# A selective scan and a quantized MLP on one core: the products by B of every fourth step of two batches move from GpSimd to TensorE

## The chip, the core and the metric

One core of a Trainium2 chip. The time of a run is the device time of the core in microseconds (us); the kernel before took 718.27 us, the median of three runs. Engines are named as in the profile: PE is TensorE (matmuls and transposes), PEld its weight loads, DVE is VectorE, ACT is ScalarE, POOL is GpSimd, SP issues the DMAs.

## What is computed

Four sequences of 512 positions, 512 channels. A block of the Mamba kind reads `ctx_1024` and is gated by the normalized `x`; its result is added to `x`, and then an MLP with quantized activations and ternary weights follows. The part that this change touches is the scan:

```python
x = silu(conv(ctx @ in_proj_w.T) + conv_b)               # u: [4, 512 channels, 512 positions]
dt_low, B, C = split(x_proj_w @ x, [16, 16, 16])         # B, C: [4, 16, 512]
dt = softplus(dt_proj_w @ dt_low + dt_proj_b)
A = -exp(A_log)                                          # [512 channels, 16 n]
state = state * exp(dt * A) + (dt * u) * B               # for each channel and n, along the positions
y = sum over n of state * C
x = x + tanh(g_xattn) * (y + D * u) * silu(layernorm(x))
x = x + tanh(g_ffn) * bitlinear(silu(bitlinear(n, w1)) * bitlinear(n, w2), w3)   # n = layernorm(x)
```

## The kernel before

The scan is cut into 128 steps, 32 to a batch; step k works on one block of 128 x 1024 numbers. In batches 0 and 1 a block is 128 channels, two n and all 512 positions. Batches 2 and 3 are "split" (`SPLIT`): a block is 128 channels, four n and half of the positions (256); the first 16 steps of such a batch do the first half, and `where_split` tells which half h, which group of channels q and which four n, k % 4 being the number of the four. In the second half a scan is issued in four pieces that start from the kept state `hl`.

A step has five stages, each on one engine:

- `times_b` (POOL, L680 in split batches, L686 else): dt*u times B into one of six buffers `hh`. It waits until `sums` of the step six before has read that buffer (`s_sum`).
- `exp` (ACT, L708 in split batches, L713 else): exp(dt*A) into one of two PSUM buffers `dbank` ("da"). It waits until the scan of the step two before has read it (`s_scan`). In the first half of a split batch column 0 of each of the four rows is zero; it is written once per buffer (L705).
- `scan` (DVE, L735 in pieces, L738 whole): reads da and hh, writes hh in place.
- `times_c` (POOL, L752 in split batches, L757 else): hh times C, in place.
- `sums` (PE, L787): eight transposes of hh by the identity, added up in `bank_y`; at the first step of a group the product D * u is added (L778). `gate` (DVE, L561, L570) then takes `bank_y`.

No scheduler orders the work. Each engine runs a loop over 125 slots that is written out by hand; the number of the slot says what each engine issues: in slot k POOL does `times_c(k)` and `times_b(k + 4)`, ACT `exp(k + 4)`, DVE `scan(k + 3)`, PE `sums(k - 1)`, each in its place among the other work. An engine goes through its instructions in order, so a wait holds back all that is behind it.

The other work is the front of the next batch (projection, convolution: L227, L302, L389 to L406), `dt_scalar` (ACT, softplus, with an ACT table load before it and another before the next exp), `du_vector` (DVE, L327) for a pair of groups in the slots of `PAIR`, the gates z, and above all the MLP of 128 rows each, the tiles. A tile starts in slot u (`tile_slot`), every six slots from slot 70 on. Its path over the engines is: rows centred (ACT, L845) and scaled (DVE, L856 and what follows; ACT, L887), transposed (PE, L904; ACT, L911), then in slots u to u + 3 for each of four chunks c `ab_tensor` (PE, L936, L942), tanh (ACT, L956), two products (DVE, L963, L971) and a square (ACT, L977). From slot u + 4 on: maximum (DVE, L1002), a power on POOL (L1033), scaling (ACT, L1029); in slots u + 8 and u + 9 `ht_tensor` turns a piece (PE, L1080), `hqt_scalar` copies it out of the one bank `bank_t` (ACT, L1091), four times in turn; in slot u + 10 `out_tensor` (PE, L1111) and `out_vector` (DVE, L1118). `ab_tensor(c + 1)` waits for the first DVE product of chunk c.

Of the places of slots one matters below: slot u + 3 of a tile holds, on PE, `sums`, then `ht_tensor` 2 and 3 of the tile before, then `ab_tensor` of chunk 3 (slots 79, 91, 103 and 115 are such slots).

## Time and profile before

| what | value |
|---|---|
| median of three runs | 718.27 us (718.25 to 718.8) |
| the profiled execution: its own time | 717.76 us |
| its span, first to last instruction | 716.0 us |
| mean granted clock of TensorE | 0.889 of full speed |
| POOL busy | 625.4 us (87%), 300 instructions |
| DVE busy | 605.9 us (85%), 839 instructions |
| ACT busy | 515.4 us (72%), 971 instructions |
| PE busy | 512.1 us (72%), 2562 matmuls |

The span is 1.76 us shorter than the time of the same execution, and that execution is 0.51 us under the median. Times in the rows below count from the first instruction of the span. A PE row's "x4" counts records: a matmul on float32 leaves two, a transpose or an fp8 matmul one.

The two split batches are steps 64 to 127; in this execution they run from about 356 us (the first `times_c` of step 64 starts at 354.8) to 669 us. What follows until 716 us is the end of the last three tiles, with no scan in it.

### The profile page before, as it was taken

The page shows a single profiled execution, that of the slowest core. Times are in us where ns is not written, and L with a number is a line of the kernel's source. Part 1 is how long each engine was busy: PE and PEld are TensorE (multiplying, and loading weights), DVE is VectorE, ACT ScalarE, POOL GpSimd, SP SyncE. Part 2 cuts the span into 40 slices and gives each one's busy share as a digit, 9 for nine tenths or more (in the row PEclk, how much of TensorE's full clock was granted, in tenths as well). Part 3 has the DMA queues.
Part 4 walks back from the last instruction along what each step waited for, and adds up shares of the span by engine and source line. Part 5 has one row for each costly group of instructions (what it writes and reads, how often), then busy time and mean ns, then how long its engine had stood idle before and what let it go on. Part 6 is the DMA issues. An engine that isn't in the chain of part 4 may idle for free.

```text
span 716.0 us, 8124 instructions
## 1 busy us (share of the span) xinstructions
PE 512.1 (72%) x2562; PEld 314.2 (44%) x2562; DVE 605.9 (85%) x839; ACT 515.4 (72%) x971; POOL 625.4 (87%) x300
## 2 busy tenths in 40 slices
PE   9787889556451758787575668578686876758897
PEld 3243434223441435555353435345453544445554
DVE  7679778977999898988868888999889889888865
ACT  5844866159867868868677777898788797677653
POOL 1499999979999999999999999988998899988431
PEclk9999999969556998999785979899999998989999
DMA  4695875258950000037310000027510000000001
GB/s 169 217 402 209 305 293 211 89 181 333 413 238 15 6 29 2 29 125 266 125 61 19 31 0 16 1 82 250 197 70 6 15 2 16 0 16 16 1 16 44
DMA packets 23930, 80.78 MB, mean 113 GB/s; under 512 B 2432, under 2 KB 4608, under 8 KB 20816
## 3 DMA queue, kind: packets, MB, share of 16 engines
q1 hardware_dynamic: 23888, 80.27, 30.7%
q8 instruction: 20, 0.33, 0.2%
q14 instruction: 22, 0.18, 0.1%
HBM read 72.53 MB, written 7.73 MB: 112 GB/s over the span
## 4 chain that ended last, share of the span: by engine, by line
DVE 29%; ACT 21%; PE 21%; POOL 13%; issue 11%; DMA 3%; SPq 1%; DVEq 0%; ACTq 0%; POOLq 0%
DVE hh L738 7%; ACT da L708 5%; DVE hh L735 4%; POOL hh L686 4%; POOL hh L757 4%; PE bank_y L787 3%; PE bank_a L936 3%; PE bank_t L1080 3%; DMA wq<-x 2%; PE bank_b L942 2%; POOL hh L680 2%; POOL hh L752 2%; ACT room L1091 2%; DVE sm L640 2%; ACT room L977 2%
## 5 line engine op out<-in xcount | busy, mean ns | idle before, releaser
L738 DVE TENSOR_TENSOR_SCAN hh<-da,hh 128x1024 f32<-128x1024 f32 x96 | 217.5, 2277 | 6.7 <-POOL hh L686 3.5
L787 PE MATMUL bank_y<-ident,hh 128*128 128x128 f32 x1024 | 146.4, 293 | 25.0 <-POOL hh L757 19.3
L757 POOL TENSOR_TENSOR hh<-hh,cc 128x1024 f32<-128x1024 f32 x64 | 160.3, 2505 | 2.4 <-DVE hh L738 2.4
L787 PEld LDWEIGHTS bank_y<-ident,hh 128*128 128x128 f32 x1024 | 130.0, 152 | 54.9 <-POOL hh L757 27.9
L752 POOL TENSOR_TENSOR hh<-hh,cc 128x1024 f32<-128x1024 f32 x64 | 151.3, 2364 | 3.1 <-ACT hl L721 2.0
L686 POOL TENSOR_TENSOR hh<-pair,bb 128x1024 f32<-128x1024 f32 x30 | 71.6, 2388 | 26.0 <-DMA bb<-xd_scratch 25.8
L735 DVE TENSOR_TENSOR_SCAN hh<-da,hl,hh 128x256 f32<-128x256 f32 x128 | 85.0, 728 | 0.0
L680 POOL TENSOR_TENSOR hh<-wq,bb 128x1024 f32<-128x1024 f32 x32 | 75.6, 2361 | 10.7 <-PE bank_y L787 10.7
L686 POOL TENSOR_TENSOR hh<-wq,bb 128x1024 f32<-128x1024 f32 x32 | 76.6, 2395 | 3.4 <-PE bank_y L787 3.4
L680 POOL TENSOR_TENSOR hh<-pair,bb 128x1024 f32<-128x1024 f32 x32 | 75.6, 2363 | 3.4 <-PE bank_y L787 3.4
L302 PE MATMUL bank_b<-room 128*128 128x512 f32 x96 | 47.4, 640 | 24.8 <-DVE wq L406 23.2
L713 ACT ACTIVATE da<-wq,cst 128x511 f32<-128x511 f32 x64 | 41.5, 684 | 28.4 <-DVE hh L738 28.3
L708 ACT ACTIVATE da<-wq,cst 128x256 f32<-128x256 f32 x128 | 53.3, 466 | 11.7 <-DVE hh L735 9.4
L708 ACT ACTIVATE da<-pair,cst 128x255 f32<-128x255 f32 x128 | 53.1, 463 | 10.9 <-DVE hh L738 10.9
L713 ACT ACTIVATE da<-pair,cst 128x511 f32<-128x511 f32 x64 | 41.3, 680 | 22.8 <-DVE hh L738 22.8
L1091 ACT ACTIVATE room<-bank_t,sm 128x512 bf16<-128x512 f32 x53 | 36.2, 683 | 28.5 <-PE bank_t L1080 28.4
L963 DVE SCALAR_TENSOR_TENSOR room<-room,bank_a 128x512 f32<-128x512 f32 x52 | 35.4, 681 | 24.5 <-ACT room L956 23.9
L936 PE MATMUL bank_a<-wq,room 128*128 128x512 fp8e4 x120 | 36.6, 434 | 16.6 <-DVE room L963 16.4
L956 ACT ACTIVATE room<-bank_a,sm 128x512 f32<-128x512 f32 x58 | 39.3, 677 | 11.3 <-PE bank_a L936 11.3
L1111 PE MATMUL bank_t<-wq,room 128*128 128x512 fp8e4 x192 | 43.4, 379 | 0.0
L936 PE MATMUL bank_a<-wq,xqT 128*128 128x512 fp8e4 x112 | 33.8, 431 | 11.7 <-DVE room L963 10.9
L302 PEld LDWEIGHTS bank_b<-room 128*128 128x128 f32 x96 | 18.6, 204 | 46.6 <-issue 37.1
(250 smaller groups left out, 1046.5 us busy)
## 6 DMA issues: line engine op xcount, KB each, us to landing
bb<-xd_scratch SPq DMA_DIRECT2D x32, 512.0 KB, 5.2
cc<-xd_scratch SPq DMA_DIRECT2D x32, 512.0 KB, 7.7
wq<-weights SPq DMA_DIRECT2D x12, 1024.0 KB, 6.5
stage<-weights SPq DMA_DIRECT2D x8, 1024.0 KB, 6.7
xin<-x SPq DMA_DIRECT2D x4, 1024.0 KB, 5.5
room<-weights SPq DMA_DIRECT2D x4, 1024.0 KB, 9.8
u_scratch<-wq SPq DMA_DIRECT2D x6, 512.0 KB, 3.4
wq<-x SPq DMA_DIRECT2D x2, 1024.0 KB, 18.5
```

The source lines that it names most:

```text
L302: mm = pe.matmul(bank_b[:, :], diag_w[:, e, k, :], xpad[e % 2][:, k:k + L], start=(k == 0), stop=(k == TAPS - 1))
L680: ins = g_.tensor_tensor(quarters(flat(hh[k % NH])), du2[g % 4][:, HALF * (q % 2):HALF * (q % 2 + 1)].unsqueeze(1).to_broadcast([P, 4, HAL ...
L686: ins = g_.tensor_tensor(hh[k % NH][:, :, :], du2[g % 4].unsqueeze(1).to_broadcast([P, GN, L]), bb[:, s * GN:(s + 1) * GN, :], ALU.mult)
L708: ins = act.activation(da[:, j, first:HALF], dt2[g % 4][:, HALF * (q % 2) + first:HALF * (q % 2 + 1)], ACT.Exp, scale=a_neg[:, q, n + j:n ...
L713: ins = act.activation(dbank[k % 2][:, j, 1:L], dt2[g % 4][:, 1:L], ACT.Exp, scale=a_neg[:, q, s * GN + j:s * GN + j + 1])
L735: ins = v.tensor_tensor_scan(h[:, t], flat(dbank[k % 2])[:, t], h[:, t], hl[:, q, n + j:n + j + 1], ALU.mult, ALU.add)
L738: ins = v.tensor_tensor_scan(h, flat(dbank[k % 2]), h, 0.0, ALU.mult, ALU.add)
L752: ins = g_.tensor_tensor(quarters(flat(hh[k % NH])), quarters(flat(hh[k % NH])), cc[:, n:n + 4, t], ALU.mult)
L757: ins = g_.tensor_tensor(hh[k % NH][:, :, :], hh[k % NH][:, :, :], cc[:, s * GN:(s + 1) * GN, :], ALU.mult)
L787: mm = pe.matmul(bank_y[:, (first + c) * P:(first + c + 1) * P], flat(hh[k % NH])[:, at:at + P], ident[:, :], start=False, stop=(s == STEP ...
L936: mm = pe.matmul(a[:, :], xqT[i % 2][:, k, :], w1q[:, k, c * 512:(c + 1) * 512], start=(k == 0), stop=(k == NE - 1))
L1091: MA.did(act.activation(hqT[:, 4 * g:4 * g + 4, :].rearrange("p a b -> p (a b)"), bank_h(i, g)[:, :], ACT.Identity, bias=nmagic), ("hqT", ...
```

## The change

In both split batches the steps with k % 4 = 3 (the n from 12 to 15, 16 steps in all) get their product dt*u*B from PE:

- `times_b` is not issued for these steps; PE does `times_b_tensor` at the start of the slot k - 4, ahead of `sums`. It is four float32 matmuls into `dbank`, 256 columns each: the stationary operand is dt*u turned (positions by channels), the moving one two diagonal matrices of B.
- `exp` of these steps goes into the buffer `hh`, and the scan reads the exponentials from `hh` and the product from `dbank`. `exp` therefore waits for `sums` of six steps before, not for the scan of two steps before. The matmuls wait for that scan (`s_scan, k - 1`).
- Each group g from 8 on is turned once (`TURN`): four PE transposes into `bank_b` or `bank_a`, one ACT copy to SBUF. The buffer of one turned group is one of the four of u; u is then loaded one group at a time into three.
- The diagonals (`DIAG`): 32 ACT copies of the identity, 128 x 128, each scaled by a column of B, into the place in `bb` that held rows 12 to 15 of the broadcast B; these rows are loaded no more (four DMAs of 512 KB less). The columns of B come from four transposes and a small ACT copy per batch (`cols`).
- Column 0 is zeroed again in every odd step of a first half.
- The softplus of groups 10 and 11 moves from slot 66 to slot 69.

The core of the diff:

```diff
-PAIR = {2: 25, 3: 37, 4: 49, 5: 66, 6: 87, 7: 99}
+PAIR = {2: 25, 3: 37, 4: 49, 5: 69, 6: 87, 7: 99}
+LAST_N = NS - 4
+TURN = {8: 62, 9: 64, 10: 75, 11: 81, 12: 93, 13: 93, 14: 105, 15: 111}
+DIAG = {(2, 0): (60, 60, 60, 61, 61, 61, 62, 62), (2, 1): (64, 65, 66, 67, 68, 69, 70, 71),
+        (3, 0): (80, 81, 82, 83, 84, 85, 86, 87), (3, 1): (96, 97, 98, 99, 100, 101, 102, 103)}
+def by_tensor(k):
+    return split(k) and k % 4 == 3
...
+        def diagonal_scalar(act, b, h, i):
+            n, c = LAST_N + i % 4, 2 * h + i // 4
...
+            CA.did(act.activation(bb[:, n, c * P:(c + 1) * P], ident[:, :], ACT.Copy,
+                                  scale=b_cols[b][:, c, i % 4:i % 4 + 1]), ("diag", b, h, i))
...
+        def turn_tensor(pe, g):
+            pe.wait_ge(*GV.of(("du", g)))
...
+            for c in range(NE):
+                mm = pe.transpose(turn_bank(g)[:, c * P:(c + 1) * P], du2[g % 4][:, c * P:(c + 1) * P], ident[:, :])
+            CP.did(mm, ("duT", g))
+        def turn_scalar(act, g):
+            act.wait_ge(*CP.of(("duT", g)))
...
+            CA.did(act.activation(duT[g % 2], turn_bank(g)[:, :], ACT.Copy), ("duT", g))
+        def times_b_tensor(pe, k):
+            b, h, q, n = where_split(k)
+            g = k // STEPS
+            pe.wait_ge(s_scan, k - 1)
+            pe.wait_ge(*CA.of(("duT", g)))
+            pe.wait_ge(*CA.of(("diag", b, h, 7)))
+            for c in range(2):
+                at = 2 * (q % 2) + c
+                for j in range(2):
+                    mm = pe.matmul(dbank[k % 2][:, j, :].rearrange("p (n t) -> p n t", n=2)[:, :, c * P:(c + 1) * P],
+                                   duT[g % 2][:, at * P:(at + 1) * P],
+                                   bb[:, n + 2 * j:n + 2 * j + 2, HALF * h + c * P:HALF * h + (c + 1) * P],
+                                   start=True, stop=True)
+            CP.did(mm, ("m1", k))
...
         def exp(act, k):
-            if k >= 2:
+            if by_tensor(k):
+                act.wait_ge(s_sum, k - NH + 1)
+            elif k >= 2:
                 act.wait_ge(s_scan, k - 1)
...
-                da = quarters(flat(dbank[k % 2]))
-                if k % PER < 2:
+                da = quarters(flat(hh[k % NH] if by_tensor(k) else dbank[k % 2]))
+                if h == 0 and (k % PER < 2 or k % 2):
                     act.activation(da[:, :, 0], zero4[:, :], ACT.Copy)
...
         def scan(v, k):
+            elif by_tensor(k):
+                v.wait_ge(*CP.of(("m1", k)))
...
+            da, m1_ = (h, flat(dbank[k % 2])) if by_tensor(k) else (flat(dbank[k % 2]), h)
...
-                    if k + LEAD < ALL:
+                    if k + LEAD < ALL and not by_tensor(k + LEAD):
                         times_b(g_, k + LEAD)
...
                 for k in range(SLOTS):
+                    if by_tensor(k + LEAD):
+                        times_b_tensor(pe, k + LEAD)
                     if 0 <= k - 1 < ALL:
                         sums(pe, k - 1)
```

How it moves instructions, in three places. First PE in slots 90 and 91, which are slots u + 2 and u + 3 of the tile that starts in slot 88 (`xqT1` is its turned input, `room` and `wq` are the tile before and the weights; `hh5` and `hh0` are `sums` of steps 89 and 90). Before:

```order
L787 MATMUL bank_y<-ident,hh5 128x128 x8
L1080 MATMUL bank_t<-ident,room 128x128 x8
L936 MATMUL bank_a<-wq,xqT1 128x512 x4
L942 MATMUL bank_b<-wq,xqT1 128x512 x4
L787 MATMUL bank_y<-ident,hh0 128x128 x8
L1080 MATMUL bank_t<-ident,room 128x128 x8
L936 MATMUL bank_a<-wq,xqT1 128x512 x4
```

Now:

```order
L876 MATMUL bank_y<-ident,hh5 128x128 x8
L1172 MATMUL bank_t<-ident,room 128x128 x8
L1028 MATMUL bank_a<-wq,xqT1 128x512 x4
L1034 MATMUL bank_b<-wq,xqT1 128x512 x4
L390 MATMUL da1<-bb,wq 128x2x128 x4
L876 MATMUL bank_y<-ident,hh0 128x128 x8
L1172 MATMUL bank_t<-ident,room 128x128 x8
L1028 MATMUL bank_a<-wq,xqT1 128x512 x4
```

The four matmuls of L390 (step 95) stand between chunk 2 of the tile and all that PE does in slot 91; the row with x8 after `sums` is `ht_tensor` 2 and 3.

Second, POOL around the same slots. Before, `times_c` of steps 90 to 92 (L752) and `times_b` of steps 94 to 96 (L680; step 95 goes into hh5):

```order
L752 TENSOR_TENSOR hh0<-hh0,cc 128x1024
L680 TENSOR_TENSOR hh4<-wq,bb 128x1024
L752 TENSOR_TENSOR hh1<-hh1,cc 128x1024
L680 TENSOR_TENSOR hh5<-wq,bb 128x1024
L752 TENSOR_TENSOR hh2<-hh2,cc 128x1024
L680 TENSOR_TENSOR hh0<-pair,bb 128x1024
```

Now:

```order
L841 TENSOR_TENSOR hh0<-hh0,cc 128x1024
L764 TENSOR_TENSOR hh4<-wq,bb 128x1024
L841 TENSOR_TENSOR hh1<-hh1,cc 128x1024
L841 TENSOR_TENSOR hh2<-hh2,cc 128x1024
L764 TENSOR_TENSOR hh0<-pair,bb 128x1024
```

`times_b(95)` is gone; `times_c` of steps 91 and 92 stand next to each other.

Third, ACT in slots 82 to 84: the scaled columns and rows of the next tile (L845; L934 now), the copy L532 (L616 now), then a tanh and an exp for each slot. Before:

```order
L845 ACTIVATE gbuf<-room,sm 128x512 x2
L532 ACTIVATE gbuf<-bank_t,sm 128x512
L956 ACTIVATE room<-bank_a,sm 128x512
L708 ACTIVATE da1<-wq,cst 128x256 x4
L1029 ACTIVATE wq<-wq,sm 128x1024 x2
L977 ACTIVATE room,sm<-room 128x512
L956 ACTIVATE room<-bank_a,sm 128x512
```

Now:

```order
L934 ACTIVATE gbuf<-room,sm 128x512 x2
L616 ACTIVATE gbuf<-bank_t,sm 128x512
L354 ACTIVATE bb<-ident,sm 128x128
L1048 ACTIVATE room<-bank_a,sm 128x512
L794 ACTIVATE hh3<-wq,cst 128x256 x4
L1121 ACTIVATE wq<-wq,sm 128x1024 x2
L1069 ACTIVATE room,sm<-room 128x512
L354 ACTIVATE bb<-ident,sm 128x128
L1048 ACTIVATE room<-bank_a,sm 128x512
```

A diagonal (L354) stands at the end of each of these slots, ahead of the next tanh; the exponentials of step 87 go to hh3.


## Rows read from the trace of the kernel before

**Rows 1.** The page's busy time of each engine over the whole span: us (share), instructions.

```profile
PE 512.1 (72%) x2562; PEld 314.2 (44%) x2562; DVE 605.9 (85%) x839; ACT 515.4 (72%) x971; POOL 625.4 (87%) x300
```

**Rows 2.** Stretches: length, then PE, PEld, DVE, ACT, POOL busy (count), clock, DMA share, GB/s.

```profile
330.00:477.00 147.00, 100.64 (x559) 67.71 (x557) 124.52 (x188) 112.77 (x252) 144.09 (x67) 0.84 0.15 50
356.00:667.00 311.00, 222.14 (x1248) 146.12 (x1248) 271.60 (x433) 246.54 (x544) 291.80 (x137) 0.89 0.13 46
574.10:577.50 3.40, 3.03 (x8) 1.11 (x9) 3.20 (x3) 3.40 (x7) 3.40 (x3) 0.50 0.02 5
```

**Rows 3.** Waits from 356 to 667 us: who waited for whom, us, times, longest.

```profile
DVE room L963 <- ACT room L956: 15.1, 17, 1.5
POOL hh L680 <- PE bank_y L787: 14.1, 9, 3.4
ACT da L708 <- DVE hh L735: 9.4, 6, 2.7
...
DVE wq L327 <- ACT bank_a L319: 5.9, 1, 5.9
PE bank_y L787 <- POOL hh L752: 4.1, 1, 4.1
DVE sm L1016 <- POOL sm L1033: 1.3, 1, 1.3
```

**Rows 4.** The chain that ended last, 356 to 667 us, its largest shares by engine and line.

```profile
by line: issue 13.0%; ACT da L708 11.1%; DVE hh L735 10.2%; POOL hh L680 5.1%; POOL hh L752 4.9%; PE bank_t L1080 4.0%; PE bank_a L936 3.6%; PE bank_y L787 3.5%; ACT room L1091 3.3%; ACT room L977 3.2%; ACT room L956 3.0%; DVE hh L738 2.9%;
```

**Rows 5.** The chain in order of time, in slots 78, 79 and 82: start, us, what.

```profile
428.88 1.71 PE bank_b L942 x4
430.58 1.01 PE bank_y L787 x8
...
450.26 0.58 ACT room L956
```

**Rows 6.** Groups, 356 to 667 us: count, busy us, mean ns of one, idle before.

```profile
L680 POOL TENSOR_TENSOR hh<-wq,bb 128x1024 f32<-128x1024 f32 x32 | 75.6, 2361 | 10.7 <-PE bank_y L787 10.7
L708 ACT ACTIVATE da<-pair,cst 128x255 f32<-128x255 f32 x112 | 46.5, 463 | 7.2 <-DVE hh L738 7.2
L505 ACT ACTIVATE gbuf<-xin,sm 128x256 f32<-128x256 f32 x16 | 9.5, 592 | 0.2
L506 ACT ACTIVATE bank_a<-xin,sm 128x256 f32<-128x256 f32 x16 | 8.9, 553 | 0.0
L532 ACT ACTIVATE gbuf<-bank_t,sm 128x512 f32<-128x512 f32 x8 | 5.3, 668 | 0.0
L705 ACT ACTIVATE da<-zero 128x4 f32<-128x4 f32 x2 | 0.4, 176 | 1.1 <-DVE hh L735 1.1
```

**Rows 7.** The same view of the whole span: exponentials of 511 columns.

```profile
L713 ACT ACTIVATE da<-pair,cst 128x511 f32<-128x511 f32 x64 | 41.3, 680 | 22.8 <-DVE hh L738 22.8
```

**Rows 8.** PE in order of time: four float32 matmuls of 256 columns, then the next.

```profile
365.51 1.03 PE L276 MATMUL bank_a<-wq,dtw 128*128 128x256 f32 x4
366.38 1.03 PE L276 MATMUL bank_b<-wq,dtw 128*128 128x256 f32 x4
367.24 0.38 PE L1111 MATMUL bank_t<-wq,room 128*128 128x512 fp8e4 x1
```

**Rows 9.** DVE, PE and ACT in order of time, in slots 90, 91 and 107.

```profile
490.34 2.67 DVE L735 TENSOR_TENSOR_SCAN hh<-da,hl,hh 128x256 f32<-128x256 f32 x4
...
492.93 1.03 PE L942 MATMUL bank_b<-wq,xqT 128*128 128x512 fp8e4 x4
...
494.67 0.60 PE L1080 MATMUL bank_t<-ident,room 128*128 128x128 f32 x4
...
494.04 1.67 ACT L708 ACTIVATE da<-wq,cst 128x256 f32<-128x256 f32 x4
495.64 0.68 ACT L1091 ACTIVATE room<-bank_t,sm 128x512 bf16<-128x512 f32 x1
...
574.47 1.89 PE L936 MATMUL bank_a<-wq,room 128*128 128x512 fp8e4 x4 [2.42 <-DVE room L963]
```

More of the change, by code:

```diff
@@ L156, in build @@
         gates = cst[:, 92:94]
-        col = iter(range(280))
+        col = iter(range(312))
         def small(n=1):
@@ L175, in build @@
         amh, amh_end = small(2), small(3)
+        b_cols = {b: small(16).rearrange("p (a b) -> p a b", a=NE) for b in SPLIT}
         am1, ss1, v2, rh, rk, amhx, ri2, csh = [small() for _ in range(8)]
@@ L193, in build @@
         HA = line("state_scalar")
+        CP, CA = line("turned_tensor"), line("turned_scalar")
         BV, BP = line("first_products"), line("first_rows_of_b")
@@ L312, in x_dbl_scalar, with cols_tensor, cols_scalar @@
             FA.did(act.activation(xd[0:ROWS, :], bank_t[0:ROWS, :], ACT.Copy), ("xd", b))
+        def cols_tensor(pe, b):
+            pe.wait_ge(*FA.of(("xd", b)))
+            for c in range(NE):
+                mm = pe.transpose(bank_t[:, c * P:(c + 1) * P], xd[:, c * P:(c + 1) * P], ident[:, :])
+            FP.did(mm, ("cols", b))
+        def cols_scalar(act, b):
+            act.wait_ge(*FP.of(("cols", b)))
+            FA.did(act.activation(b_cols[b], bank_t[:, :].rearrange("p (a b) -> p a b", a=NE)[
+                :, :, RANK + LAST_N:RANK + NS], ACT.Copy), ("cols", b))
@@ new lines, in turn_bank @@
+        def turn_bank(g):
+            return bank_a if g == 13 else bank_b
+        def turn_tensor(pe, g):
+            pe.wait_ge(*GV.of(("du", g)))
+            if g == 9:
+                pe.wait_ge(*CA.of(("duT", g - 1)))
+            else:
+                tile = max(i for i in range(END) if tile_slot(i) < TURN[g])
+                pe.wait_ge(*MV.of(("g" if g == 13 else "h", tile, NCH - 1)))
+            for c in range(NE):
+                mm = pe.transpose(turn_bank(g)[:, c * P:(c + 1) * P], du2[g % 4][:, c * P:(c + 1) * P], ident[:, :])
+            CP.did(mm, ("duT", g))
@@ new lines, in turn_scalar @@
+        def turn_scalar(act, g):
+            act.wait_ge(*CP.of(("duT", g)))
+            if g == 2 * NE:
+                act.wait_ge(*d_bw.of(("bw", NB - 1)))
+            elif g == 2 * NE + 1:
+                act.wait_ge(s_seed, 2 * NE)
+            else:
+                act.wait_ge(*CP.of(("m1", STEPS * (g - 2) + 7)))
+            CA.did(act.activation(duT[g % 2], turn_bank(g)[:, :], ACT.Copy), ("duT", g))
[13 more added lines that the diff above has]
+            CP.did(mm, ("m1", k))
@@ L663, in m1_done @@
         def m1_done(k):
-            return k - 1
+            return k - 1 - sum(by_tensor(i) for i in range(k + 1))
         def times_b(g_, k):
@@ L923, in ab_tensor @@
                     pe.wait_ge(*GV.of(("du", 2 * pair_before(i) + 1)))
+                for g in TURN:
+                    if 0 < i <= END and tile_slot(i - 1) < TURN[g] < tile_slot(i):
+                        pe.wait_ge(*CA.of(("duT", g)))
             if i == END and c == 1:
@@ L1139, in weight_part, with u_before, load_u @@
                     return weights[i // 4][:, (i % 4) * WC:(i % 4 + 1) * WC]
[L1141 to L1145 removed]
+                def u_before(g):
+                    return g - 3 if g > 2 * NE + 2 else g - NE
+                def load_u(g):
+                    b, n = g // NE, g // 2
+                    sp.wait_ge(s_seed, u_before(g) + 1)
+                    sp.wait_ge(*GV.of(("du", u_before(g))))
                     for half in d_uw:
                         sp.wait_ge(*half.of(b))
[L1148 to L1154 removed]
+                    if b in SPLIT:
+                        h, p = n % 2, g % 2
+                        d_u[n % 2].did(sp.dma_start(u_of(g).rearrange("p (a b) -> p a b", a=2),
+                                                    u_dram[b, :, 2 * p:2 * p + 2, HALF * h:HALF * (h + 1)]), n)
+                    else:
+                        d_u[n % 2].did(sp.dma_start(u_of(g), u_dram[b, :, g % NE, :]), n)
                 def load_dt_rows(b):
@@ L1225, in _ @@
                             load_dt_rows(b)
-                    for n in PAIR:
-                        if k == 16 * n - 20:
-                            load_u(n)
+                    for g in range(NE, NB * NE):
+                        if k == (8 * g - 20 if g % 2 == 0 else 8 * g - 28 if g < 10 else 8 * g - 22):
+                            load_u(g)
                     for i in range(NW):
@@ L1255, in _ @@
                         for s in range(STEPS):
-                            if k == last_use(b - 1, s) - LEAD + 1:
+                            if k == last_use(b - 1, s) - LEAD + 1 and not (b in SPLIT and s >= LAST_N // GN):
                                 load_bb(b, s)
@@ L1350, in _ @@
                             x_dbl_scalar(act, b)
+                        if k == FRONT[b] + 10 and b in SPLIT:
+                            cols_scalar(act, b)
                     for i in range(NW):
@@ L1385, in _ @@
                             z_turn_scalar(act, i)
+                    for g in TURN:
+                        if k == TURN[g]:
+                            turn_scalar(act, g)
+                    for b, h in DIAG:
+                        for i in range(8):
+                            if k == DIAG[b, h][i]:
+                                diagonal_scalar(act, b, h, i)
                     if k == 9:
@@ L1471, in _ @@
                             out_tensor(pe, i)
+                    for b in SPLIT:
+                        if k == FRONT[b] + 10:
+                            cols_tensor(pe, b)
                     for i in TILES:
@@ L1474, in _ @@
                             z_turn_tensor(pe, i)
+                    for g in TURN:
+                        if k == TURN[g]:
+                            turn_tensor(pe, g)
                     for i in range(END + 1):
```

42 lines of the change are left out of this document (22 added, 20 removed).

## The prediction

> **What bounds the kernel now.** The busy shares come first [rows 1]: POOL leads with 87%, DVE follows with 85%, so on that view the change takes work from the right engine. The two split batches are the stretch from 356 to 667 us [rows 2]: POOL is busy 291.8 of 311 us (94%), DVE 271.6 (87%), ACT 246.5 (79%), PE 222.1 (71%). The reader is to see two things there: POOL has hardly any idle time, and no engine below it has much either.
>
> A busy engine need not be a waited-for engine, so the waits come next [rows 3]. In these 311 us DVE waits for POOL once, 1.3 us, in the power of a tile, not in a scan. PE waits for POOL once, 4.1 us. POOL in turn waits 14.1 us in nine places for `sums` on PE, before just the instruction that the change removes. DVE's long waits are on ACT (15.1 us in 17 places before the first product of a chunk), and ACT's on DVE. POOL runs without gaps because its buffers let it follow, not because others stand in line for it.
>
> The chain that ended last says the same by another road [rows 4]: of the named shares POOL has 5.1 + 4.9 = 10.0% of 311 us, 31 us; ACT, DVE and PE share nearly all the rest in turn. My reading: **the tile path over PE, ACT and DVE, tied to the scans by program order, sets the end of the split batches, and POOL keeps up with it.** So what is taken from POOL is worth little, and what is put on PE or ACT counts where the chain passes.
>
> **The change part by part.** The sum is made against the profiled execution, 717.76 us; the median of the runs shown lies 0.51 us above it.
>
> *Products off POOL.* 16 instructions of 2.36 us [rows 6] are 37.8 us less on POOL. What others wait for POOL is 1.3 and 4.1 us [rows 3], so the gain is between 0 and 5.4 by that view; the far end is rival A. I take 1.3: PE, after its wait of 4.1, has no tile work ready. **-1.3.**
>
> The Trainium skill has a rule that would give another sum: its page Perfetto Trace Analysis, section Identifying the Most-Contended Engine, takes the engine of highest occupancy as the bottleneck, to be relieved first. By that rule this step alone would give the gain of rival A, and the trace, in which the others hardly wait for this engine, speaks against it.
>
> *Products on PE.* Four float32 matmuls of 256 columns. L276 does the same four in 367.24 - 365.51 = 1.73 us, at full clock [rows 8]. 16 times this is 27.7 us more on PE; at the lower clock, twice that. The bounds on the path are 0 and 27.7 (55 with every one at half clock). Where they stand on the path: in slot 79 the chain goes on PE from `ab_tensor` straight to `sums` [rows 5], and the products go between: +1.73. In slot 91 `ht_tensor` 2 ends at 494.67 + 0.60 = 495.27 and ACT takes it at 495.64, after its exponentials [rows 9]; with 1.73 ahead it ends at 497.00, and the copy, `ht_tensor` 3, chunk 3 and its tanh come 1.36 later. Slots 103 and 115 have the same pattern. 1.73 + 3 x 1.36 = **+5.8**. In the other slots PE's next tile work waits for something that ends later, so I take nothing. The wait for the scan does not bind in slot 91: that scan ends at 490.34 + 2.67 = 493.01, PE is free at 492.93 + 1.03 = 493.96 [rows 9]. Behind the products on PE stand `sums`, the transposes and chunk 3; for `sums` POOL waits, which now has 2.36 us to spare.
>
> *Clock.* From 574.1 to 577.5 the granted clock is 0.50, that is 1.2 GHz [rows 2]; before it PE waits 2.42 us for DVE, and the four matmuls then take 1.89 us, against 1.03 for four of the kind in slot 90 [rows 9]. In slot 107 the products fill this gap: chunk 1 starts about 0.8 later and, if the clock stays up, ends about 1.6 sooner over its two banks. **-0.8**; the bounds are +0.8 and, should several such stretches go, some -4.
>
> *Diagonals.* 511 columns take 680 ns [rows 7], 255 take 463 [rows 6]: 0.85 ns a column, so 128 columns are about 355 ns. Four exponentials follow each other in 1.67 us [rows 9], some 0.06 us each less than their records; a diagonal holds ACT for about 0.30. Eight stand in slots 60 to 62, before the stretch; 24 stand in it, 0 to 8.5 us. On the path: where the chain stays on ACT past the end of a slot, as from slot 82 to 83 [rows 5]; I count six such ends. 6 x 0.30 = **+1.8**.
>
> *Small additions on ACT.* 14 more zeroings of 176 ns [rows 6], of which three on the path: +0.5. Exponentials into SBUF: a 256-column activation takes 592 ns there and 553 into PSUM [rows 6], so 64 x 0.04 = 2.5 us at most; I take 0.5. Eight copies of a turned group at 668 ns [rows 6], and as many times four transposes at 0.60 [rows 9]: 0 to 10; most fall where ACT waits for a scan, I take one copy, 0.7. Together **+1.7**.
>
> *At nothing.* The wait of 16 `exp` on a scan goes; a quarter of 9.4 us [rows 3] would be 2.4, but in slot 91, the pattern slot, `exp` starts as soon as tanh is done, so the scan is not what ends its wait. The next thing that could be late is the scan itself, which now waits for PE: products done at about 495.7 in slot 91, a slot ahead of their scan. The softplus of groups 10 and 11 moves three slots: DVE's wait of 5.9 us for it [rows 3] goes from its place and comes back three slots on, with the same table loads; 0, bounds -5 and +3. The columns of B are small, and four DMAs fewer relieve queues that nothing here waits for.
>
> Sum: -1.3 + 5.8 - 0.8 + 1.8 + 1.7 = +7.2, so 725.0 for the profiled execution and **725.5** for the median.
>
> **The rivals.**
>
> *A, faster: POOL is the bound after all.* Place: 330 to 477 us, where POOL is busy 144.1 of 147 us and DVE has 22 us to spare [rows 2]. Mechanism: the chain shows only the wait that ends last; DVE and ACT may run at just POOL's pace because everything is tied through `sums` and the buffers. Six of the sixteen products were issued there, in slots 63 to 83: 6 x 2.36 = 14.2 us, hence 703.6, a median near 704. It decides if additions to PE and ACT stay below about 7 us on the path and DVE can use the time. For it: the near-absence of gaps on POOL. Against it: one wait on POOL of 1.3 us on DVE's side, none in a scan worth the name.
>
> *B, much slower: PE becomes the bound.* Each group of products stands at the head of a slot and waits for a scan, so the transposes and chunks behind it slip each time; 12 more of them at 1.73 on the path are +20.8, about 746. It decides if the slip of one slot is still there when the next product comes, four slots on. Against it: PE is at 71% and has its own gaps.
>
> *C, no change.* The relief in the stretch of A and the additions after it cancel: 718 within 1.4 us. For it: both sums are of like size.
>
> **How the numbers follow.** About 0.2% (1.4 us) is what a measurement of this kernel can tell from no change. Forecast 0.46, A 0.33, B 0.08, C 0.13. Faster 0.33; same 0.13; slower 0.46 + 0.08 = 0.54. The range: upward the forecast's own, where products, diagonals and turned groups take about half of their upper bounds, to 737; it leaves out B. Downward A, with some room below its 704, to 702; it leaves out the tenth in which more than six products pay. The likeliest case's own range is 719 to 737.
>
> **What would show it.** Right: POOL's busy time falls by about 38 us and its idle time in the split batches grows by as much or more; that stretch gets no shorter; on the chain POOL's share falls, and L390 (products) and L354 (diagonals) appear between PE and ACT pieces; in slots u + 3 the copy after `ht_tensor` 2 comes over a microsecond later than tanh and exponentials would allow. Products take about 1.73 us a group at full clock. Wrong: steps between 330 and 477 us at well under the 4.7 us of two POOL operations [rows 6], which would be A; or scans that wait for L390, which I have put at nothing; or stretches at half clock that vanish in numbers.

## The result and the profile after

The changed kernel takes 729.87 us, median of four executions (726.21 to 730.86), beside 718.26 us for the kernel before on the same chip: a ratio of 1.0153 [1.0135, 1.0171]. It is slower, by 11.6 us; the prediction was 725.5 us in a range of 702 to 737, with slower the likeliest outcome. A second set of six executions (run 10) has a median of 726.25 us, 7.9 us over the kernel before; all ten together have 727.9. The profiled execution is one of 730.16 us, its span 728.4 us, the mean granted clock 0.892.

The page's busy times, which answer to [rows 1]:

```profile
PE 545.4 (75%) x2730; PEld 345.4 (47%) x2730; DVE 607.1 (83%) x839; ACT 530.6 (73%) x1027; POOL 589.1 (81%) x284
```

POOL is busy 36.3 us less, PE 33.3 us and ACT 15.2 us more, DVE as before. The stretches follow, with the columns of [rows 2]: first the split batches, then three stretches at half clock.

```profile
356.00:679.00 323.00, 248.99 (x1394) 173.19 (x1393) 270.38 (x430) 258.38 (x587) 255.29 (x120) 0.91 0.12 42
453.30:460.10 6.80, 6.08 (x18) 4.70 (x19) 5.44 (x13) 6.33 (x13) 2.21 (x2) 0.50 0.00 0
525.00:531.80 6.80, 5.93 (x20) 3.88 (x21) 6.44 (x7) 4.78 (x14) 4.21 (x2) 0.50 0.26 92
555.70:562.50 6.80, 5.58 (x19) 3.46 (x20) 6.26 (x10) 6.15 (x14) 5.12 (x3) 0.50 0.00 0
```

The split batches took 311 us and take 323. In them POOL is busy 255.3 us instead of 291.8, so its idle time grew from 19 to 68 us, and nothing came of it. The waits of that stretch (who for whom: us, times, longest) show where it sits, beside [rows 3]:

```profile
POOL hh L764 <- PE bank_y L876: 51.8, 21, 4.9
DVE room L1055 <- ACT room L1048: 28.8, 19, 3.4
ACT room L1183 <- PE bank_t L1172: 28.3, 27, 2.7
...
ACT da L794 <- DVE hh L824: 6.6, 5, 2.3
PE da L390 <- DVE hh L827: 6.3, 3, 3.5
...
DVE hh L827 <- PE da L390: 0.5, 1, 0.5
```

POOL's wait for `sums` on PE went from 14.1 to 51.8 us: all that was taken from POOL became waiting for PE. DVE's wait for tanh on ACT in front of a chunk went from 15.1 to 28.8, and ACT's wait for transposes on PE (`ht`, L1172; L1080 before) went from 20.1 to 28.3. A scan waits for the products (L390) once, 0.5 us. The chain that ended last, by line, against [rows 4]:

```profile
by line: DVE hh L824 10.0%; issue 9.6%; PE bank_y L876 6.2%; ACT da L794 5.9%; PE bank_a L1028 5.3%; PE da L390 4.7%; PE bank_t L1172 4.6%; DVE hh L827 4.2%; POOL hh L841 3.8%; PE bank_b L1034 3.8%; ACT room L1183 3.3%; DVE sm L1094 2.8%; P
```

Products on TensorE have 4.7% of 323 us there, 15 us; they are busy for 36.1 us in all (L390 below), so some two fifths of their time is on the path. The groups of the whole span that are new, with POOL's remaining products (columns as in [rows 6]):

```profile
L764 POOL TENSOR_TENSOR hh<-wq,bb 128x1024 f32<-128x1024 f32 x24 | 56.5, 2353 | 32.6 <-PE bank_y L876 32.6
...
L390 PE MATMUL da<-bb,wq 128*128 128x256 f32 x128 | 36.1, 431 | 15.3 <-DVE hh L827 6.3 <-ACT bb L354 5.5 <-DVE hh L824 3.5
...
L794 ACT ACTIVATE hh<-wq,cst 128x256 f32<-128x256 f32 x32 | 13.6, 497 | 0.0
L354 ACT ACTIVATE bb<-ident,sm 128x128 f32<-128x128 f32 x32 | 12.0, 391 | 0.0
```

A product on POOL kept its length, 2353 ns. A diagonal takes 391 ns, an exponential of 256 columns into SBUF 497 ns, where one of 255 into PSUM takes 463 [rows 6].

**Where the time arises.** The same scan can be found in both traces. The start of scan k, us from the start of the span, at the places where the lag jumps:

```
scan      before  after    lag
 69       364.4   365.2    0.82
 74       394.2   396.1    1.87
 82       431.3   433.2    1.88
 83       436.8   440.5    3.74   products of slot 79
 86       452.4   456.2    3.84
 87       457.2   462.8    5.61   products of slot 83
 94       495.5   501.1    5.57
 95       500.4   507.3    6.98   products of slot 91
100       524.0   531.1    7.07
101       528.9   538.4    9.46   525.0 to 531.8 at half clock
105       551.8   561.5    9.75
106       556.8   567.9   11.16   555.7 to 562.5 at half clock
107       561.7   574.2   12.48   products of slot 103
111       580.0   592.6   12.57
112       585.0   598.5   13.54   593.3 to 596.7 at half clock
118       617.0   629.8   12.74
119       621.9   636.0   14.15   products of slot 115
127       664.1   677.6   13.54
```

The four slots of the prediction give 1.9 + 1.4 + 1.3 + 1.4 = 6.0 us, where it had 1.73 + 3 x 1.36 = 5.8. The chain in order of time in slot 91 (start, us, what) shows the mechanism as it was put:

```profile
498.67 0.86 PE bank_b L1034 x4
499.53 1.73 PE da L390 x8
501.26 0.87 PE bank_y L876 x8
502.13 0.45 PE bank_t L1172 x4
...
502.61 0.70 ACT room L1183
```

The products stand between chunk 2's second bank and `sums`, and the copy of the tile's turned piece on ACT (L1183) comes behind all of it. Three other jumps, 1.8 + 2.4 + 1.4 = 5.6 us, were not in the prediction, and half clock is in each. Of the rest, 0.8 us stand before scan 69, and 1.1 us up to scan 74 have no cause shown (run 5); the 1.0 us at scan 112 is for the greater part gone by scan 118. In slot 83:

```profile
451.29 2.69 DVE hh L824 x4
...
454.02 3.78 PE da L390 x8
457.80 1.71 PE bank_y L876 x8
459.51 1.26 PE bank_a L1028 x4
...
460.80 0.70 ACT room L1048
```

The products wait for the scan, then take 3.78 us, where those of slot 91 take 1.73; `sums` takes 1.71 instead of 0.87, and chunk 1 behind it is late too. In slots 96 and 97 no product stands on the chain at all:

```profile
525.87 1.09 PE bank_t L1172 x4
526.96 1.71 PE bank_a L1028 x4
528.66 1.71 PE bank_b L1034 x4
530.37 1.65 PE bank_y L867 x8
```

Transposes, both banks of a chunk and the product D * u (L867) run at half clock, 1.71 us for a bank that takes 0.86 in slot 91. The kernel before has full clock in the same place, which is some 7 us earlier there:

```profile
517.60:524.40 6.80, 4.82 (x32) 3.40 (x32) 6.73 (x8) 5.11 (x14) 6.80 (x4) 1.00 0.19 65
```

### The profile page after: what moved, and what is told of

It is laid out like the page before. It is cut to its first block, busy times and chain, and to the rows that moved or that the text cites. A ratio compares the mean times of both kernels' runs of the same rounds, so it can differ in the third digit from the quotient of the medians.

```text
span 728.4 us, 8552 instructions
## 1 busy us (share of the span) xinstructions
PE 545.4 (75%) x2730; PEld 345.4 (47%) x2730; DVE 607.1 (83%) x839; ACT 530.6 (73%) x1027; POOL 589.1 (81%) x284
## 4 chain that ended last, share of the span: by engine, by line
DVE 29%; PE 27%; ACT 17%; POOL 13%; issue 9%; DMA 3%; SPq 1%; DVEq 0%; ACTq 0%; POOLq 0%
DVE hh L827 7%; POOL hh L846 5%; POOL hh L770 5%; PE bank_y L876 5%; DVE hh L824 4%; PE bank_a L1028 4%; PE bank_t L1172 3%; PE bank_b L1034 3%; ACT da L794 3%; PE da L390 3%; DMA wq<-x 2%; ACT room L1183 2%; DVE sm L724 2%; POOL hh L841 2%; DVE sm L1094 2%
## 5 line engine op out<-in xcount | busy, mean ns | idle before, releaser
L827 DVE TENSOR_TENSOR_SCAN hh<-da,hh 128x1024 f32<-128x1024 f32 x88 | 199.6, 2277 | 6.4 <-POOL hh L770 3.6
L876 PE MATMUL bank_y<-ident,hh 128*128 128x128 f32 x1024 | 145.7, 292 | 15.2 <-POOL hh L846 13.6
L770 POOL TENSOR_TENSOR hh<-pair,bb 128x1024 f32<-128x1024 f32 x30 | 71.6, 2389 | 26.5 <-DMA bb<-xd_scratch 24.9
L764 POOL TENSOR_TENSOR hh<-wq,bb 128x1024 f32<-128x1024 f32 x24 | 56.5, 2353 | 32.6 <-PE bank_y L876 32.6
L770 POOL TENSOR_TENSOR hh<-wq,bb 128x1024 f32<-128x1024 f32 x32 | 76.8, 2400 | 2.6 <-PE bank_y L876 2.6
L764 POOL TENSOR_TENSOR hh<-pair,bb 128x1024 f32<-128x1024 f32 x24 | 56.5, 2354 | 19.3 <-PE bank_y L876 19.3
L824 DVE TENSOR_TENSOR_SCAN hh<-da,hl,hh 128x256 f32<-128x256 f32 x96 | 63.9, 729 | 0.0
L1183 ACT ACTIVATE room<-bank_t,sm 128x512 bf16<-128x512 f32 x53 | 36.3, 685 | 35.4 <-PE bank_t L1172 35.3
L1048 ACT ACTIVATE room<-bank_a,sm 128x512 f32<-128x512 f32 x58 | 39.3, 677 | 11.9 <-PE bank_a L1028 11.7
L390 PE MATMUL da<-bb,wq 128*128 128x256 f32 x128 | 36.1, 431 | 15.3 <-DVE hh L827 6.3
L794 ACT ACTIVATE da<-wq,cst 128x256 f32<-128x256 f32 x96 | 39.9, 466 | 6.7 <-DVE hh L824 6.6
L794 ACT ACTIVATE da<-pair,cst 128x255 f32<-128x255 f32 x96 | 39.8, 462 | 6.6 <-DVE hh L827 6.5
L1028 PE MATMUL bank_a<-wq,xqT 128*128 128x512 fp8e4 x112 | 33.3, 426 | 11.9 <-DVE room L1055 11.6
```

Of the source, the lines that this page charges most:

```text
L390: mm = pe.matmul(dbank[k % 2][:, j, :].rearrange("p (n t) -> p n t", n=2)[:, :, c * P:(c + 1) * P], duT[g % 2][:, at * P:(at + 1) * P], bb ...
L764: ins = g_.tensor_tensor(quarters(flat(hh[k % NH])), du2[g % 4][:, HALF * (q % 2):HALF * (q % 2 + 1)].unsqueeze(1).to_broadcast([P, 4, HAL ...
L770: ins = g_.tensor_tensor(hh[k % NH][:, :, :], du2[g % 4].unsqueeze(1).to_broadcast([P, GN, L]), bb[:, s * GN:(s + 1) * GN, :], ALU.mult)
L794: ins = act.activation(da[:, j, first:HALF], dt2[g % 4][:, HALF * (q % 2) + first:HALF * (q % 2 + 1)], ACT.Exp, scale=a_neg[:, q, n + j:n ...
L824: ins = v.tensor_tensor_scan(h[:, t], da[:, t], m1_[:, t], hl[:, q, n + j:n + j + 1], ALU.mult, ALU.add)
L827: ins = v.tensor_tensor_scan(h, da, m1_, 0.0, ALU.mult, ALU.add)
```

## The experiments

Each ran beside the kernel before, whose median was 718.4 to 718.5 us in every set; ratios are to it.

**1. POOL's relief alone.** From the kernel before:

```diff
+def left_out(k):
+    return split(k) and k % 4 == 3
...
-            return k - 1
+            return k - 1 - sum(left_out(i) for i in range(k + 1))
...
+            elif left_out(k):
+                v.wait_ge(s_sum, k - NH + 1)
...
-                    if k + LEAD < ALL:
+                    if k + LEAD < ALL and not left_out(k + LEAD):
```

> The kernel before with the 16 products simply left out on POOL and nothing put in their place (these steps scan what their buffer still holds; the scan waits for sums in their stead). This prices the relief by itself. If POOL only follows the tile path: 1.3 us faster, at most 5.4, so 713 to 718, near 717. If POOL is the bound (rival A): about 14 us faster, near 704.

Measured: 719.28 us, ratio 1.0013 [1.0, 1.0026]: no gain. The split batches and three of their waits:

```profile
356.00:667.00 311.00, 221.94 (x1238) 148.27 (x1239) 269.79 (x430) 245.46 (x542) 254.29 (x120) 0.89 0.13 46
```

```profile
POOL hh L684 <- PE bank_y L793: 34.8, 20, 4.1
...
DVE room L969 <- ACT room L962: 18.0, 18, 2.0
...
DVE hh L744 <- ACT da L712: 0.6, 1, 0.6
```

POOL is busy 37.5 us less, as in the change, and waits for `sums` 34.8 us where it waited 14.1. Rival A (704 us) falls: POOL, at 94% in this stretch, is not what the kernel waits for. The time lies just over the range of the first expectation (713 to 718) and far from the second. It also shows the term of -1.3 us to be nothing. The wait that these scans were given instead hides no gain in this profile: the only wait of a scan in the stretch is one of 0.6 us, for an exponential (L744).

**2. A quarter of each product.** From the changed kernel:

```diff
-            for c in range(2):
+            for c in range(1):
...
-                for j in range(2):
+                for j in range(1):
```

> The changed kernel with one of the four matmuls of each group of products; the other three quarters of the product are left out, all waits stay. 1.30 us less of PE per group. If the time of the matmuls lies on the path at the steps where the scans fell back (in slots 79, 83, 91, 103 and 115 by 1.3 to 1.9 us each, 7.8 together): three quarters of that come back, about 6 us, near 724. If it is the wait of PE for the scan, and not its work, that costs: no change, 729 to 731.

Measured: 720.99 us, ratio 1.0036 [1.0023, 1.0049]: 9 us come back, more than the 6 of the theory (5 us against the second set of the change, run 10). So the time on PE is the greater part of the cost, not the waits, copies or diagonals that stay. Its mean granted clock was 0.888 to 0.898, as low as the change's. That does not clear the clock, for its half-clock stretches are placed otherwise: in its profile they last 3.4 us and not 6.8 in slot 83 and in slots 96 and 97, and the jumps there are 0.5 and 1.4 us instead of 1.8 and 2.4. The run takes away work on PE and half clock in these places together.

**3. The products later in their slots.** From the changed kernel, nothing left out:

```diff
-                    if by_tensor(k + LEAD):
-                        times_b_tensor(pe, k + LEAD)
+                    later = by_tensor(k + LEAD)
...
+                            if later:
+                                times_b_tensor(pe, k + LEAD)
+                                later = False
...
+                    if later:
+                        times_b_tensor(pe, k + LEAD)
```

> The changed kernel, the products moved back within their slot on PE: behind transposes 2 in slots 79, 91, 103 and 115, at the end of the slot in the twelve others. Nothing left out. If their place at the head of the slot is what costs: in slots 83 and 119 chunk 1 no longer stands behind them (1.8 and 1.3 back), in the four others the gap of 1.2 us between transposes 2 and 3 takes most of it (0.8 each back): about 5 us, near 725. If PE's amount of work costs, wherever it stands: no change. If the scans then wait for products: slower than 730.

Measured: 720.88 us, ratio 1.0031 [1.0019, 1.0043]: again 9 us back, with all of the products kept (5 us against the second set of the change). What is left over the kernel before is 2.4 us. Place decides: the same work costs 5 to 9 us more at the head of a slot.

**4. Small diagonals.** From the changed kernel:

```diff
-            CA.did(act.activation(bb[:, n, c * P:(c + 1) * P], ident[:, :], ACT.Copy,
+            CA.did(act.activation(bb[:, n, c * P:c * P + 4], ident[:, 0:4], ACT.Copy,
```

> The changed kernel with diagonals of 4 columns and not 128 (the rest of each diagonal matrix is left out). ACT is held about 0.1 us and not 0.3 by each of the 24 in the split batches. With six of them on the path, as counted before: 1.2 us faster, near 728.5. With all on the path: 4.8 us, near 725.

Measured: 728.68 us, ratio 1.014 [1.0122, 1.0158], 1.2 us under the change's median. The group shows what was saved:

```profile
L354 ACT ACTIVATE bb<-ident,sm 128x4 f32<-128x4 f32 x32 | 8.7, 286 | 0.0
```

286 ns in place of 391, 3.4 us over 32, so most of a diagonal's length is fixed. The gain has the expected size, but the intervals overlap, and run 10 shows the changed kernel itself at 725.4 to 731.6: on the diagonals this one is inconclusive.

Its trace is of use for something else, for all sixteen products stand in it at full length at the head of their slots. Its lag is 2.9 us at scan 64 already, ahead of the split batches, against 0.9 in the change's profile; from scan 74 to scan 127 it grows by 8.8 us, and in the change by 11.7. The stretches at half clock in the places of the three extra jumps:

```profile
455.40:458.80 3.40, 2.98 (x7) 2.45 (x8) 3.26 (x10) 3.40 (x8) 1.39 (x1) 0.50 0.00 0
527.10:530.40 3.30, 3.30 (x13) 2.34 (x12) 3.23 (x5) 3.18 (x11) 2.02 (x1) 0.50 0.13 33
554.40:561.20 6.80, 5.71 (x19) 3.57 (x20) 6.40 (x9) 5.70 (x13) 5.00 (x3) 0.50 0.00 0
```

In the first two places half clock lasts 3.4 us and not 6.8, and the jumps (scans 87 and 101) are 0.4 and 1.3 us instead of 1.8 and 2.4. In the third it lasts as long as in the change, and the jump (scan 106) is 1.4 us in both. So the extra jumps go with the length of the half clock there, with the same products ahead; that the shorter diagonals have a part in it is not ruled out.

**5. The softplus moved alone.** From the kernel before:

```diff
-PAIR = {2: 25, 3: 37, 4: 49, 5: 66, 6: 87, 7: 99}
+PAIR = {2: 25, 3: 37, 4: 49, 5: 69, 6: 87, 7: 99}
...
-                    pe.wait_ge(*ZV.of(("zz", {3: 4, 4: 6, 5: 7, 6: 11, 7: 12}[n])))
+                    pe.wait_ge(*ZV.of(("zz", {3: 4, 4: 6, 5: 8, 6: 11, 7: 12}[n])))
```

> The kernel before, with the softplus pair that the change moves from slot 66 to slot 69 moved alone (and its wait for the z of the next tile); nothing left out. The prediction put this move at 0, with bounds of -5 and +3. The changed kernel's scans gain 4 us at scans 70 to 72 and lose 5 until scan 74, a net of about +1. Theory (a small loss, which belongs to the change): 718.5 to 720, nearest 719.5. Rival (the loss at scan 74 is due to what PE and ACT do there in the changed kernel, and the move by itself is worth nothing or saves some of the 4 us): 714 to 718.

Measured: 718.19 us, ratio 0.9996 [0.9985, 1.0008]. My theory of a small loss falls; the 0 of the prediction stands. The lag of +1.1 us between scans 69 and 74 is not a price of this move: in this run's trace the lag is 1.7 us at scan 69 and 1.6 at scan 74. Where it comes from stays open.

**6. Only four groups later.**

```diff
-                    if by_tensor(k + LEAD):
+                    later = by_tensor(k + LEAD) and k in (79, 91, 103, 115)
+                    if by_tensor(k + LEAD) and not later:
                         times_b_tensor(pe, k + LEAD)
```

(with the lines of run 3 behind the third turn)

> The changed kernel with the products of four slots only (79, 91, 103 and 115, in which PE also turns the third and fourth part of a tile) put behind the third turn; the other twelve groups stay at the head of their slots. Nothing left out. Theory by the prediction's own terms (these four are the 5.8 us): 729.9 - 5.8 = about 724, and what is left to the 720.9 of the kernel with all sixteen put later is the twelve that were taken at nothing (3 us). Rival (the four cost what the scans' steps show, but what they give back is lost in the next tile work, and the twelve matter most): 727 or more.

Measured: 720.42 us, ratio 1.0049 [1.0024, 1.0074]. The interval is wide because the twelve executions lie in two groups: seven of 718.4 to 720.5 us at a mean granted clock of 0.907 to 0.910, five of 724.1 to 726.5 at 0.896 to 0.899. The quicker group is no slower than run 3: there the other twelve products cost nothing at the head of their slots, as the prediction took it. The other five executions are 3 to 6 us over run 3's median, so this does not hold in all of them. The profile is of the quicker group:

```profile
356.00:669.00 313.00, 240.30 (x1397) 167.61 (x1396) 270.64 (x431) 257.68 (x587) 256.03 (x120) 0.93 0.13 43
451.60:455.00 3.40, 3.26 (x8) 2.63 (x9) 3.25 (x10) 3.40 (x8) 1.12 (x1) 0.50 0.00 0
455.00:458.40 3.40, 3.40 (x24) 2.41 (x23) 2.06 (x4) 3.40 (x8) 2.13 (x1) 1.00 0.01 2
519.80:526.60 6.80, 4.82 (x32) 3.40 (x32) 6.73 (x8) 5.50 (x15) 5.43 (x3) 1.00 0.28 75
```

Slot 83's products stand at its head here too (451.7 us) and take 3.57 us at half clock, but full clock is back at 455.0, 3.4 us after it fell and not 6.8; the lag grows by 0.5 us instead of 1.8. The place of slots 96 and 97 (519.8) has full clock, and the jump of 2.4 us is not there.

**7 and 8. Using POOL's freed time.** The rounding of eight tiles (`hq`) from ACT to POOL, on run 3's kernel and on the kernel before:

```diff
+ROUND_POOL = range(4, 12)
...
-                pe.wait_ge(*(MG if at_end(i) or i == END - 1 and g >= 2 else MA).of(("hq", i, g // 2)))
+                pe.wait_ge(*(MG if at_end(i) or i == END - 1 and g >= 2 or i in ROUND_POOL else MA).of(("hq", i, g // 2)))
...
+                    for i in ROUND_POOL:
+                        if k == tile_slot(i) + 7:
+                            hq_pool(g_, i, 0)
+                            hq_pool(g_, i, 1)
...
-                        if k == u + 7:
+                        if k == u + 7 and i not in ROUND_POOL:
```

> The changed kernel with the products put later (720.9), and besides, the rounding of eight tiles (16 ScalarE instructions of 128x1024, 1.23 us each) done by POOL (1.12 us each by the five at the end), at the end of the same slot. Nothing left out. It uses the time that the change freed on POOL (about 37 us) to free 19.7 us on ScalarE. Theory (ScalarE and the chain through it carry a good part of the rest, and POOL has room): 20 to 40 per cent of 19.7 us come back, so 713 to 717, nearest 715, which is under the kernel before. Rival (ScalarE waits for PE in these slots anyway, 21 us before its copies of turned tiles, and the round comes later from POOL because POOL is in the middle of a product): 720 to 724.

> The kernel before with the same rounding of eight tiles done by POOL in place of ScalarE; nothing left out. Here POOL is busy 94 per cent of this stretch and idle for only 19 us, so 18 us more on it leave no slack. Theory (POOL has no room without the change, so the freed time of POOL is what the move needs): POOL becomes the bound and it takes 3 to 10 us more, 721 to 728. Rival (the load on POOL does not decide, as leaving out 38 us of it did not, and the relief of ScalarE is worth the same with and without the change): 712 to 716.

Measured: 717.77 us, ratio 0.9989 [0.9976, 1.0002], with the change; 721.3 us, ratio 1.0039 [1.0024, 1.0054], without it. The same move saves 3 us on the one and costs 2.9 on the other. The chain of the second, 356 to 668 us, and two POOL groups of it:

```profile
by line: POOL hh L753 21.4%; POOL hh L681 19.2%; issue 13.5%; DVE hh L736 9.4%; ACT da L709 4.3%; PE bank_a L937 2.3%; PE bank_t L1081 2.2%; ACT room L1092 1.7%; DVE room L964 1.7%; PE bank_b L943 1.5%; DVE sm L1003 1.5%; POOL wq L1040 1.4%
```

```profile
L681 POOL TENSOR_TENSOR hh<-wq,bb 128x1024 f32<-128x1024 f32 x32 | 75.5, 2358 | 0.0
L1040 POOL TENSOR_SCALAR room<-room,sm 128x1024 f32<-128x1024 f32 x8 | 8.9, 1122 | 3.2 <-DVE sm L1024 3.2
```

Now POOL's two products have 40.6% of the chain, against 10.0% in the kernel before [rows 4], and their idle time for `sums` (10.7 us, [rows 6]) is 0. So 18 us more on POOL make it the bound, though 37.5 us less gave nothing: it was close to being one, and was none. With the change the same groups have room:

```profile
L765 POOL TENSOR_TENSOR hh<-wq,bb 128x1024 f32<-128x1024 f32 x24 | 56.6, 2357 | 4.1 <-PE bank_y L877 4.1
L1132 POOL TENSOR_SCALAR room<-room,sm 128x1024 f32<-128x1024 f32 x8 | 8.9, 1119 | 9.9 <-DVE sm L1116 9.9
```

With the change the time lies between the theory's range (713 to 717) and the rival's, so the theory's size was too good; POOL waits 9.9 us for the scales in front of these eight roundings, and 11.0 in front of the other eight.

**9. Less of it, and more.** Rounding on POOL for tiles 5, 7, 9 and 11 alone (`ROUND_POOL = (5, 7, 9, 11)`), and then the diagonals on POOL too:

```diff
-            CA.did(act.activation(bb[:, n, c * P:(c + 1) * P], ident[:, :], ACT.Copy,
-                                  scale=b_cols[b][:, c, i % 4:i % 4 + 1]), ("diag", b, h, i))
+            DG.did(g_.tensor_scalar(bb[:, n, c * P:(c + 1) * P], ident[:, :], b_cols[b][:, c, i % 4:i % 4 + 1],
+                                    None, ALU.mult), ("diag", b, h, i))
```

> The kernel with the products put later, and the rounding of four tiles (numbers 5, 7, 9 and 11) on POOL in place of all eight. These are the tiles whose rounding falls into a slot from which the change took the POOL product (83, 95, 107, 119), so there the two roundings of 1.12 us each take the place of a product of 2.36 us; the other four go back to ScalarE, for POOL waited 21 us in front of the roundings for their scales with all eight. Nothing left out. Theory (only the freed slots have room on POOL): at least as good as with all eight, 715.5 to 717.5, nearest 716.5. Rival (each of the eight pays in the same way by what it takes off ScalarE): half of the 3 us, 719 to 719.5.

> The same kernel with the 32 diagonals of B made by POOL in place of ScalarE (391 ns each there, 12.5 us; with four columns in place of 128 they cost the changed kernel 1.2 us less). Nothing left out. Theory (POOL still has room, so what the diagonals cost on ScalarE comes back): 1 to 2 us under the kernel without this, so 714.5 to 716. Rival (POOL has no more room in the slots where they fall, two or three at a time in slots 60 to 62, with its products at their full number until 66): 0 to 2 us more, 716.5 to 719.

Measured: 719.2 us, ratio 0.9998 [0.9983, 1.0013], and 720.43 us, ratio 1.0014 [0.9991, 1.0036]. By the ratios four tiles save 2.4 us against run 3 and eight 3.0, with intervals that reach 1 us to either side, so whether the freed slots are what counts stays open. The median, 719.2, lies in the rival's range (719 to 719.5) and not in the theory's. With the diagonals on POOL the median is over both ranges, and its executions lie in two groups, four of 714.6 to 716.8 us at 0.911 to 0.912 and eight of 720.0 to 722.8 at 0.903 to 0.910. No gain of the diagonals is measured there, at 609 ns each:

```profile
L355 POOL TENSOR_SCALAR bb<-ident,sm 128x128 f32<-128x128 f32 x32 | 19.4, 609 | 0.0
```

No version of these is measurably quicker than the kernel before.

**10. Only four groups first, and the change again.** The counterpart of run 6 (`k not in (79, 91, 103, 115)` for the ones put later), and more executions of the changed kernel:

> The counterpart of the last but one pair: the four groups of slots 79, 91, 103 and 115 stay at the head of their slots, as in the change, and the other twelve go to the end of theirs. Nothing left out. Theory (the four cost the 5.9 us that the scans show, and the rest of the 9 us is time at half clock, which comes and goes with where the twelve stand): 725.5 to 727.5, nearest 726.7 = 720.9 + 5.8. Rival (the four carry all of it, by whatever way): 729 to 730.5, as the changed kernel.

> The changed kernel itself, with more executions (there are four so far: 726.2 at a mean granted clock of 0.903, and 729.6 to 730.9 at 0.892 to 0.895). The kernel with four groups put later fell into two groups, seven executions of 718.4 to 720.5 at 0.907 to 0.910 and five of 724.1 to 726.5 at 0.896 to 0.899. Theory (about 5 us of a time hang on how often PE falls to half clock, in one program from execution to execution): two groups again, 4 to 5 us apart, the quicker with the higher clock, near 726 and 730.5. Rival (the 726.2 is scatter, and its clock too): one group within 2 us, with no order by clock.

Measured: 724.98 us (721.79 to 726.09), ratio 1.0088 [1.0067, 1.0109]; and 726.25 us (725.38 to 731.57), ratio 1.0127 [1.0099, 1.0155]. The four alone cost 4.1 us over run 3 (0.57% of 718.4), a little less than their 5.8 and just under the theory's range, and not the whole 9. That 9 is itself from the first set: against this set's 726.25 the change costs 5.4 us over run 3, and moving the four alone (run 6) gives back 5.8, moving the twelve alone 1.3. The order by clock has an exception in the run of the four: 725.85 us at 0.908, beside 721.8 to 724.3 at 0.907 to 0.910. The ten executions of the changed kernel over both sets lie in two groups, as the theory had it: five of 725.4 to 726.3 us, all at a mean granted clock of 0.903, and five of 729.6 to 731.6 at 0.892 to 0.897. The profile above is of the second group, and so is that of this set (730.34 us, 0.892), whose scans jump in the same places by the same amounts; of the first there is none.

## Why the prediction was right, point by point

**What bounds the kernel: right.** POOL's high share was not a bound. The waits and the chain said so ahead of the change; run 1 shows it, and run 8 shows how near the edge it was. By the rule of the Trainium skill (Perfetto Trace Analysis, Identifying the Most-Contended Engine) the relief should have paid; this case's run 1, with ratio 1.0013 at 37.5 us less on POOL, disagrees.

**Products off POOL, -1.3: nothing.** +0.9 us [0, 1.9] in run 1.

**Products on PE, +5.8: right in place, about right in size.** The four slots' jumps sum to 6.0 us in the trace. Run 3 and run 6 give back what they cost by moving them. Compared group with group, the change over run 6 is 726.2 - 719.3 = 6.9 us in the quicker groups and 730.3 - 724.9 = 5.4 in the others (middle values of each group; the clocks, 0.903 and 0.907 to 0.910 in the quicker ones, are near but not the same). "In the other slots I take nothing" holds for run 6's quicker group, which is no slower than run 3. It does not hold in the change's profile: slot 83's products, at half clock, are on the path with 1.8 us.

**Clock, -0.8: the step that was mis-sized.** The prediction let the products fill a gap and keep the clock up; its upper bound was +0.8. In the changed kernel five executions of ten are 4.1 us slower (730.3 against 726.2) at a lower mean clock, and the profile of one of them has three jumps, 5.6 us, that lie in half-clock stretches. In the trace of the prediction's own example, slot 107, nothing was gained either. Four rows of the change, and then two of the kernel before (PE in order of time):

```profile
585.23 1.99 PE L390 MATMUL da<-bb,wq 128*128 128x256 f32 x8 [1.33 <-DVE hh L827]
...
587.93 1.03 PE L1028 MATMUL bank_a<-wq,room 128*128 128x512 fp8e4 x4
588.80 1.03 PE L1034 MATMUL bank_b<-wq,room 128*128 128x512 fp8e4 x4
...
593.62 1.09 PE L1172 MATMUL bank_t<-ident,wq 128*128 128x128 f32 x4 [2.49 <-ACT room L1183]
```

```profile
576.15 1.70 PE L942 MATMUL bank_b<-wq,room 128*128 128x512 fp8e4 x4
...
581.05 0.63 PE L1080 MATMUL bank_t<-ident,wq 128*128 128x128 f32 x4 [1.89 <-ACT room L1091]
```

The products fill the gap and chunk 1 runs at full clock, as forecast, and with the lag of 12.5 us taken off it ends about 0.5 us sooner. But ACT is in two roundings (L1121, 2.36 us from 587.66; L1029 from 575.09 before) until after that, and the tanh, the exponentials and the copy that the next transposes wait for come behind them: the transposes (L1172) start 12.57 us later, just the lag. So the half microsecond gave nothing to what follows. These transposes and the chunk behind them now meet the half clock of 593.3 to 596.7, and the lag goes from 12.6 at scan 111 to 13.5 at scan 112.

That half clock causes the 4.1 us is argued from the places of the jumps, from their size in run 4 and run 6 where half clock lasts half as long, and from the order of times by clock within one program. It is not shown: no run held the clock fixed, and between programs the order fails, for run 4, with all the products in place, takes 727.9 to 729.4 us at 0.899 to 0.906.

**Diagonals, +1.8, and small additions, +1.7: not told apart.** Run 4's 1.2 us for the columns of the diagonals is inside the scatter. Run 3, with all of these additions, stands 2.4 us [1.4, 3.1] over the kernel before, so together with the rest they are not over the 3.5 by much, if at all.

**At nothing: right.** The softplus (run 5), and the scans, which wait for the products once, 0.5 us.

The sum, 725.5, falls on the quicker group of the changed kernel (725.4 to 726.3), partly by luck: -1.3 and -0.8 too good, the ACT terms perhaps too dear. The median of the first set, 729.87, is of the other group. Of the rivals, A fell with run 1. B (746) did not come: between the jumps the lag is flat, so a delay once taken stays but does not grow with each product, and of the twelve other groups only slot 83's is seen in a jump of its own, 1.8 us, and slot 107's ahead of the 1.0 at scan 112.

## What to carry to other kernels

An engine at 94% in its stretch can be worth nothing to relieve: look for who waits for it, and if in doubt leave its work out for one run. Work that is put on an engine with gaps can cost next to nothing where it stands behind what others wait for, and up to its full length where it stands ahead (here 1.3 to 1.9 us in each of four slots out of sixteen); ask for each slot, and put it last. And time freed on an engine is only worth what is then moved onto it: the same move saved 3 us with it and cost 3 without.

## What was not expected of the hardware

One and the same program has executions in two groups 4 to 6 us apart, the quicker one at the higher mean granted clock of TensorE: 726.2 us at 0.903 and 730.3 at 0.892 to 0.897 for the change, 719.3 at 0.907 to 0.910 and 724.9 at 0.896 to 0.899 for run 6. The kernel before, at a lower clock than either (0.878 to 0.889 over the four sets beside the runs), spreads over 716.0 to 720.9 us, nearly as wide, but without a gap. So the mean clock doesn't rank programs; which work falls into the half-clock stretches is what the jumps point to. A diagonal of 128x128 takes 609 ns on POOL and 391 on ACT, and of 4 columns 286 on ACT.
